# Identity products on TensorE at four waits between the attention and the expert layer of a Perceiver block

## The chip, the cores and the metric

One core of one Trainium2 chip runs the whole kernel. The metric is the device time of one execution in microseconds (us). The engines named below are TensorE (PE in the rows, PEld its weight loads), VectorE (DVE), ScalarE (ACT), GpSimd (POOL) and SyncE (SP), which issues the DMAs.

## The reference

The input x is 2 x 128 tokens of width 512, the context 2 x 2048 tokens. Three blocks follow one another, each with a residual:

```python
x = x + xattn(_layernorm(x), ctx_1024)       # 16 heads of 32, keys and values from the context
x = x + attn(_layernorm(x))                  # self-attention, its own residual and layer norm inside
x = x + ffn(_layernorm(x))                   # 4 experts, top 1
...
# attn: Q, K, V are reshaped (B, S, E) -> (B * H, S, D) without a transpose of heads
out = softmax(Q @ K.T / sqrt(D)) @ V
out = layer_norm(out @ wo + bo + x) * gamma + beta
...
# ffn
expert_idx = argmax(x @ W_router)
h = gelu(x @ W1[e] + b1[e])                  # 512 -> 2048, of the chosen expert
y = layer_norm(h @ Wo + bo + x)
```

## The kernel before

Each engine has one program, written out by hand, and waits on semaphores; nothing is reordered by a scheduler. All data lives at fixed places of SBUF, and PSUM is one array `ps` of 8 banks.

The cross-attention takes the first 356 us and is untouched. Then comes the stretch that this document is about, which has little work for each engine and many hand-overs:

1. `wo` product: TensorE multiplies `attnT` with `wo` for the two halves b of the batch (16 products of 512 columns in the trace). VectorE adds the residual and normalizes to `y`, half by half, with one `pow` on GpSimd each.
2. TensorE transposes `y` (4 per half), ScalarE copies to `yT`, and TensorE makes q, k and v of the self-attention (`qkv`, lines 778, 32 rows each in the trace).
3. Heads are regrouped by copies over 32 partitions: `QT2` by VectorE (L638), `KT2` by VectorE (L648) and ScalarE (L396), `VT2` by ScalarE (L396). `scores2` (L953) needs QT2 and KT2 only.
4. `softmax2(u)` for u = 0 to 7 on VectorE (L658, L659), `exponentials2(u)` on ScalarE (L412), `probs2_T(u)` transposes on TensorE (L963) and their copies on ScalarE (L418). In ScalarE's order the first exponential stands behind all eight VT2 copies of head groups 0 and 1, and four more copies stand behind each of the first two exponentials. Then the transposes of V (L992), `outputs2(0)` (L971, L976), reciprocals and regrouping of its result (L665, L672, L425), the `wo2` product of half 0, `outputs2(1)`, the same again for half 1, and the `wo2` product of half 1.
5. VectorE alone works through the residual, two layer norms and the residual again (L698 to L703, L490), first for half 0 and then for half 1. TensorE transposes each `y` (L772) as it comes, ScalarE copies it, and TensorE makes the router logits (L778, `wr`, 4 columns).
6. VectorE picks the expert (L710 to L717). TensorE spreads the one-hot masks over the partitions (L1024) and transposes them (L1029, `ohT`). VectorE copies `ohT` (L729) behind the splitting of the biases b1 (L725, L727).
7. The expert layer: 16 products with b1 (L1040), whose contraction has only 4 partitions (one for each expert), then 16 tiles of W1 with 24 products of 512 columns each (L1051 to L1053), which VectorE splits into high and low parts two tiles ahead. The output layer and the store follow.

At the very start of the program, TensorE already runs 14 identity products (L863) while the first inputs load; they write to bank `PV_BANK` and nothing reads them. A product of two fp32 operands stands in the trace as two MATMUL records, so these 14 are 28 records.

Of the kernel before, what the change touches and what calls it, by code (L numbers as in the profile page):

```python
# [17 lines left out]
P = 128  # L18
# [5 lines left out]
def perceiver_block(nc, a, out):  # L24
    B, T, D = a["x"].shape
# [4 lines left out]
    HPG = P // DH  # L30
# [17 lines left out]
    with ExitStack() as ctx:  # L48
# [3 lines left out]
        def at(name, shape, dtype, kb):  # L52
            return nc.alloc_sbuf_tensor_at(name, shape, dtype, offset=base + int(kb * KB))

        def sem(name):
            return ctx.enter_context(nc.semaphore(name))
# [19 lines left out]
        ident = at("ident", [P, P], F32, 204)  # L76
# [55 lines left out]
        def cols(n):  # L132
# [25 lines left out]
        ps = ctx.enter_context(nc.psum_tensor("ps", [P, 8, CH], F32))  # L158
        T_BANKS = (4, 5)
        K_BANK, PV_BANK = 6, 7  # L160
# [36 lines left out]
        ones_ready, s2_mm, sub2_done, exp2_done, p2T_mm, pt2_act = (  # L197
            sem(n) for n in ("ones_ready", "s2_mm", "sub2_done", "exp2_done", "p2T_mm", "pt2_act"))
# [569 lines left out]
        def _(pe):  # L768
            def transposes(src, b, bank, sem_out):

                for k in range(KT):
                    last = pe.transpose(ps[:, bank, k * T:(k + 1) * T], src[:, b, k * P:(k + 1) * P], ident[:])  # L772
                last.then_inc(sem_out, 1)

            def product(dst, pairs):

                for n, (l, r) in enumerate(pairs):
                    mm = pe.matmul(dst, l, r, start=(n == 0), stop=(n == len(pairs) - 1))  # L778
                return mm
# [86 lines left out]
            for k in range(KT):  # L866
                if k % HALF == 0:
                    pe.wait_ge(ctx_split, k // HALF + 1)
                for n, (w, t) in enumerate(((wkH, ctxH[0]), (wkL, ctxH[0]), (wkH, ctxL[0]))):
                    last = pe.matmul(ps[:, K_BANK, :], w[:, k, 0:P], t[:, k, :], start=(k == 0 and n == 0),  # L870
                                     stop=(k == KT - 1 and n == 2))
# [62 lines left out]
                    .then_inc(wo_mm, 1)  # L934


            pe.wait_ge(wqkv2_in, 48)
            for b in range(B):
                pe.wait_ge(norm_done, B + b + 1)
                transposes(y, b, 2 + b, yT_mm)  # L940
# [25 lines left out]
            def outputs2(b):  # L966
# [10 lines left out]
                                         start=True, stop=True)  # L977
                last.then_inc(pv2_mm, 1)

            pe.wait_ge(q2_ready, HPG * HPG)  # L980
            pe.wait_ge(k2_dve, 2 * HPG)
            pe.wait_ge(k2_act, 2 * HPG)
# [28 lines left out]


            pe.wait_ge(wr_in, 16)
            for b in range(B):
                pe.wait_ge(norm_done, 2 * B + 2 * (b + 1))
                transposes(y, b, 2 + b, x2T_mm)
                pe.wait_ge(x2T_done, b + 1)
                product(ps[:, 6 + b, 0:E], [(yT[:, k, b * T:(b + 1) * T], wr[:, k, :]) for k in range(KT)])\
                    .then_inc(logit_mm, 1)
# [10 lines left out]
            last.then_inc(ohT_mm, 1)  # L1030


            pe.wait_ge(ohT_ready, 1)
            pe.wait_ge(b1_split, 2)
            pe.wait_ge(mask_done, E // 2)
            pe.wait_ge(yT_lo, B)
            for b in range(B):
                for c in range(IC):
                    for n, part in enumerate((b1H, b1L)):
                        pe.matmul(ps[:, IC * b + c, :], ohT[:, b, :], part[:, c * CH:(c + 1) * CH],  # L1040
                                  start=(n == 0), stop=False)
# [77 lines left out]
```

## Time and profile before

| | |
|---|---|
| median of 3 runs | 601.75 us |
| lowest, highest | 601.21, 604.71 us |
| profiled execution, its whole time | 603.38 us |
| profiled execution, its span | 601.6 us |
| PE busy | 528.6 us, 88% of the span |
| DVE, ACT, POOL busy | 311.2, 184.1, 37.2 us |
| mean granted TensorE clock | 0.933 |

The span runs from the first to the last instruction of the profiled execution; 1.8 us of its whole time lie outside it. A granted clock of 1.00 is 2.4 GHz and 0.50 is 1.2 GHz. All times in the rows count from the start of the span.

### The profile page before, as it was taken

The numbers are of one execution on the slowest core, as the hardware profiler recorded it, in microseconds if no ns is written. First come the engines' busy times: TensorE is split into PE (matmuls) and PEld (weight loads), VectorE is DVE, ScalarE is ACT, GpSimd is POOL, SyncE is SP. The second block draws the span as 40 slices with busy tenths as digits, with TensorE's granted clock in tenths as the row PEclk, the third lists the DMA queues.
The fourth block names the chain that finished last, engine by engine and source line by source line (L and its number), as shares of the span: only waits on it lengthen the run. The fifth ranks groups of instructions, "written<-read, shape, count | busy, mean of one in ns | idle before, by whom it ended". The sixth has DMA issues, their size and how long they took to land.

```text
span 601.6 us, 8656 instructions
## 1 busy us (share of the span) xinstructions
PE 528.6 (88%) x3550; PEld 393.9 (65%) x3550; DVE 311.2 (52%) x561; ACT 184.1 (31%) x282; POOL 37.2 (6%) x32
## 2 busy tenths in 40 slices
PE   6999999999989899999999587934555999999995
PEld 5777767777767688777767455823225788888642
DVE  4545335566756411175757222874286579766122
ACT  3110053737363431136363720493222000000400
POOL 0300000003940000000000000000000000000000
PEclk9999999999989999999999798977765699999999
DMA  8600000004300000300004420000020565542000
GB/s 290 253 0 1 1 1 1 2 2 144 138 0 3 1 0 1 139 3 2 1 1 185 167 99 9 0 3 1 0 70 2 244 246 200 212 173 113 0 8 28
DMA packets 7998, 41.24 MB, mean 69 GB/s; under 512 B 1172, under 2 KB 2196, under 8 KB 4116
## 3 DMA queue, kind: packets, MB, share of 16 engines
q1 hardware_dynamic: 7960, 40.69, 18.3%
q8 instruction: 29, 0.48, 0.3%
q14 instruction: 9, 0.07, 0.0%
HBM read 40.16 MB, written 0.52 MB: 68 GB/s over the span
## 4 chain that ended last, share of the span: by engine, by line
PE 80%; DVE 9%; ACT 5%; issue 3%; DMA 1%; POOL 0%; SPq 0%; POOLq 0%; DVEq 0%; ACTq 0%
PE ps L778 41%; PE ps L835 10%; PE ps L821 6%; PE ps L1051 5%; PE ps L1052 5%; PE ps L1053 5%; PE ps L850 5%; ACT VT L396 2%; DMA wv_raw<-in_xWv 1%; PE ps L1040 1%; DVE rden L665 1%; DVE Pm L526 1%; DVE small L484 1%; DVE cT L672 1%; ACT Pm L325 1%
## 5 line engine op out<-in xcount | busy, mean ns | idle before, releaser
L333 ACT COPY PT<-ps 128x512 f32<-128x512 f32 x96 | 53.3, 588 | 102.0 <-PE ps L835 102.0
L835 PE MATMUL ps<-ident,Pm 128*128 128x128 f32 x512 | 71.1, 282 | 4.9 <-ACT PT L333 2.7
L835 PEld LDWEIGHTS ps<-ident,Pm 128*128 128x128 f32 x512 | 57.8, 143 | 24.9 <-issue 16.9
L526 DVE TENSOR_SCALAR_CACHE_REDUCE Pm<-ps,small 128x512 f32<-128x512 f32 x96 | 66.4, 748 | 8.6 <-PE ps L821 8.6
L325 ACT ACTIVATE Pm<-Pm,small 128x2048 f32<-128x2048 f32 x32 | 64.2, 2006 | 14.2 <-DVE Pm L526 14.2
L778 PE MATMUL ps<-ctxH,wkH 128*128 128x512 f32 x124 | 52.0, 419 | 2.8 <-DVE Kr L506 2.4
L1051 PE MATMUL ps<-w1H,zH 128*128 128x512 f32 x128 | 50.7, 396 | 0.0
L778 PE MATMUL ps<-wvH,ctxH 128*128 128x512 f32 x128 | 50.3, 393 | 0.2 <-DVE wvL L570 0.2
L1052 PE MATMUL ps<-w1L,zH 128*128 128x512 f32 x128 | 50.5, 395 | 0.0
L1053 PE MATMUL ps<-w1H,zL 128*128 128x512 f32 x128 | 50.3, 393 | 0.0
L778 PE MATMUL ps<-wvL,ctxH 128*128 128x512 f32 x128 | 50.0, 391 | 0.0
L778 PE MATMUL ps<-wvH,ctxL 128*128 128x512 f32 x128 | 50.0, 391 | 0.0
L778 PE MATMUL ps<-ctxL,wkH 128*128 128x512 f32 x124 | 49.3, 398 | 0.0
L778 PE MATMUL ps<-ctxH,wkL 128*128 128x512 f32 x124 | 49.0, 395 | 0.0
L506 DVE TENSOR_SCALAR Kr<-ps,small 128x512 f32<-128x512 f32 x32 | 24.0, 750 | 47.1 <-PE ps L778 47.1
L515 DVE COPY V<-ps 128x512 f32<-128x512 f32 x16 | 11.1, 692 | 62.7 <-PE ps L778 62.7
L535 DVE COPY PT<-ps 128x512 f32<-128x512 f32 x32 | 22.1, 692 | 36.4 <-PE ps L835 35.6
L778 PEld LDWEIGHTS ps<-ctxH,wkH 128*128 128x128 f32 x124 | 23.6, 190 | 21.5 <-issue 17.5
L821 PE MATMUL ps<-Kr,qT 32*128 32x512 f32 x256 | 36.5, 640 | 0.6 <-ACT qT L352 0.6
L690 DVE TENSOR_TENSOR w1L<-w1raw,w1H 128x2048 fp32r<-128x2048 f32 x16 | 36.7, 2293 | 0.6
L850 PE MATMUL ps<-PT,V 128*32 128x128 f32 x1024 | 34.6, 276 | 0.9 <-DVE PT L535 0.9
L320 ACT COPY V<-ps 128x512 f32<-128x512 f32 x16 | 9.4, 589 | 77.5 <-PE ps L778 77.5
(151 smaller groups left out, 718.4 us busy)
## 6 DMA issues: line engine op xcount, KB each, us to landing
w1raw<-in_W SPq DMA_DIRECT2D x16, 1024.0 KB, 4.8
raw<-in_ctxT SPq DMA_DIRECT2D x7, 1024.0 KB, 4.9
woF<-in_ffn_Wo SPq DMA_DIRECT2D x1, 4096.0 KB, 14.0
rows<-in_rows SPq DMA_DIRECT2D x6, 256.0 KB, 3.9
raw<-in_ctxT SPq DMA_DIRECT2D x2, 512.0 KB, 6.2
wv_raw<-in_xWv SPq DMA_DIRECT2D x2, 512.0 KB, 8.5
wq<-in_xWq SPq DMA_DIRECT2D x1, 1024.0 KB, 12.9
wo<-in_xWo SPq DMA_DIRECT2D x1, 1024.0 KB, 4.7
```

The lines of the kernel that those rows point to most:

```text
L325: act.activation(Pm[:, i, :], Pm[:, i, :], ACT.Exp, bias=mx[:, p % 2, i, C - 1:C], scale=-1.0, accum_out=den[:, p, i:i + 1]).then_inc(exp_ ...
L333: act.copy(PT[:, c % 2, i, :, :].rearrange("p k t -> p (k t)"), ps[:, T_BANKS[i % 2], :]).then_inc(pt_act, 1)
L506: dve.tensor_scalar(Kr[:, c, :], ps[:, K_BANK, :], bias3[:, 1, p % G:p % G + 1], None, ALU.add).then_inc(k_done, 1)
L526: dve.tensor_scalar(Pm[:, i, c * CH:(c + 1) * CH], ps[:, i, :], -1.0, mx[:, p % 2, i, c - 1:c] if c else NOT_YET, ALU.mult, ALU.min, accum ...
L690: dve.tensor_tensor(w1L[n % 2][:], w1raw[n % 2][:], w1H[n % 2][:].bitcast(F32), ALU.subtract).then_inc(w1_split, 1)
L778: mm = pe.matmul(dst, l, r, start=(n == 0), stop=(n == len(pairs) - 1))
L821: pe.matmul(ps[:, i, :], qT[q, g, b * T:(b + 1) * T], Kr[q, c, :], start=True, stop=True)\
L835: last = pe.transpose(ps[:, T_BANKS[i % 2], j * P:(j + 1) * P], Pm[:, i, c * CH + j * P:c * CH + (j + 1) * P], ident[:])
L850: last = pe.matmul(ps[q, PV_BANK, 0:T], V[:, c * JT + j, (HPG * g + i) * DH:(HPG * g + i + 1) * DH], PT[:, c % 2, i, j, :], start=(c == 0 ...
L1051: pe.matmul(dst, zH[:, n, t], wH[:, cc], start=False, stop=False)
L1052: pe.matmul(dst, zH[:, n, t], wL[:, cc], start=False, stop=False)
L1053: last = pe.matmul(dst, zL[:, n, t], wH[:, cc], start=False, stop=(n == NW1 - 1))
```

## The change

A helper `busy(n)` issues n products of the 128x128 identity with itself into `PV_BANK`, columns 0 to 127. They signal nothing. It is called four times on TensorE:

- 16 products behind the `wo` product, after the wait for the weights `wq2`, `wk2`, `wv2` and ahead of the wait for `y` (call 1);
- 40 products behind q, k and v, ahead of the waits for QT2 and KT2 (call 2);
- 40 products behind the last `wo2` product, after the wait for the router's weights and a further wait for `pt2_act` (the bank holds the last transposed probabilities until ScalarE has copied them; the same count was already awaited ahead of `outputs2(1)`), and ahead of the wait for the normalized tokens (call 3);
- 40 products behind the one-hot transposes, ahead of the waits for `ohT`, b1 and the masks (call 4).

```diff
@@ -934,7 +934,12 @@
+            def busy(n):
+                for _ in range(n):
+                    pe.matmul(ps[:, PV_BANK, 0:P], ident[:], ident[:], start=True, stop=True)
+
             pe.wait_ge(wqkv2_in, 48)
+            busy(16)
             for b in range(B):
                 pe.wait_ge(norm_done, B + b + 1)
                 transposes(y, b, 2 + b, yT_mm)
@@ -977,6 +982,7 @@
                 last.then_inc(pv2_mm, 1)
 
+            busy(40)
             pe.wait_ge(q2_ready, HPG * HPG)
             pe.wait_ge(k2_dve, 2 * HPG)
             pe.wait_ge(k2_act, 2 * HPG)
@@ -1011,6 +1017,8 @@
             pe.wait_ge(wr_in, 16)
+            pe.wait_ge(pt2_act, B * HPG)
+            busy(40)
             for b in range(B):
                 pe.wait_ge(norm_done, 2 * B + 2 * (b + 1))
                 transposes(y, b, 2 + b, x2T_mm)
@@ -1030,6 +1038,7 @@
             last.then_inc(ohT_mm, 1)
 
+            busy(40)
             pe.wait_ge(ohT_ready, 1)
             pe.wait_ge(b1_split, 2)
             pe.wait_ge(mask_done, E // 2)
```

The other engines' programs stay as they are. On TensorE, calls 1 and 2 stand around q, k and v; before:

```order
L778 MATMUL ps<-wo,attnT 128x512 x8
L772 MATMUL ps<-ident,y 128x128 x8
L778 MATMUL ps<-yT,wq_82 128x256 x16
L778 MATMUL ps<-yT,wk_83 128x256 x16
L778 MATMUL ps<-yT,wv_84 128x256 x16
L953 MATMUL ps<-KT_107,QT_106 128x128 x32
```

and now (the scores have moved from L953 to L958 of the file):

```order
L778 MATMUL ps<-wo,attnT 128x512 x8
L939 MATMUL ps<-ident 128x128 x16
L772 MATMUL ps<-ident,y 128x128 x8
L778 MATMUL ps<-yT,wq_82 128x256 x16
L778 MATMUL ps<-yT,wk_83 128x256 x16
L778 MATMUL ps<-yT,wv_84 128x256 x16
L939 MATMUL ps<-ident 128x128 x40
L958 MATMUL ps<-KT_107,QT_106 128x128 x32
```

Everything behind an inserted group on TensorE waits for it to be issued. Calls 3 and 4 stand around the router, again on TensorE; before:

```order
L778 MATMUL ps<-wo_85,cT 128x512 x4
L772 MATMUL ps<-ident,y 128x128 x4
L778 MATMUL ps<-wr,yT 128x4 x4
L1024 MATMUL ps<-ident,small 128x128 x8
L1029 MATMUL ps<-ident,small 4x128 x2
L1040 MATMUL ps<-b1H,ohT 128x512
```

and now:

```order
L778 MATMUL ps<-wo_85,cT 128x512 x4
L939 MATMUL ps<-ident 128x128 x40
L772 MATMUL ps<-ident,y 128x128 x4
L778 MATMUL ps<-wr,yT 128x4 x4
L1032 MATMUL ps<-ident,small 128x128 x8
L1037 MATMUL ps<-ident,small 4x128 x2
L939 MATMUL ps<-ident 128x128 x40
L1049 MATMUL ps<-b1H,ohT 128x512
```

One group now precedes the transposes of half 0 and one the products with b1; the pair of transposes and logits for half 1, not shown twice, has no group ahead of it.

## Rows read from the trace of the kernel before

**Rows 1.** The page: engines' busy time, and the granted clock in 40 slices.

```profile
PE 528.6 (88%) x3550; PEld 393.9 (65%) x3550; DVE 311.2 (52%) x561; ACT 184.1 (31%) x282; POOL 37.2 (6%) x32
...
PEclk9999999999989999999999798977765699999999
```

**Rows 2.** Timeline of TensorE, the 28 identity records at the start.

```profile
start us, us, engine line op out<-in xcount [idle before <-releaser]
1.52 4.42 PE L863 MATMUL ps<-ident 128*128 128x128 f32 x19 [1.52 <-POOL ident L272]
...
5.52 1.49 PE L863 MATMUL ps<-ident 128*128 128x128 f32 x10
```

**Rows 3.** Windows of the stretch: busy time of each engine, granted clock (PEclk).

```profile
core 0: us, PE busy (x) PEld busy (x) DVE busy (x) ACT busy (x) POOL busy (x), PEclk, DMA share, GB/s
...
363.41:367.70 4.29, 1.29 (x9) 0.81 (x8) 2.27 (x5) 0.84 (x2) 0.55 (x1) 1.00 0.02 4
367.80:371.10 3.30, 3.01 (x7) 2.48 (x8) 0.00 (x0) 0.24 (x1) 0.00 (x0) 0.50 0.00 0
...
398.60:408.70 10.10, 5.53 (x25) 4.61 (x24) 4.84 (x8) 9.03 (x17) 0.00 (x0) 0.50 0.00 0
408.75:415.50 6.75, 3.25 (x75) 2.60 (x73) 3.36 (x1) 2.23 (x5) 0.00 (x0) 1.00 0.01 2
415.60:429.15 13.55, 5.62 (x10) 2.67 (x11) 4.05 (x11) 5.38 (x12) 0.00 (x0) 0.50 0.00 0
...
446.30:449.60 3.30, 0.65 (x3) 0.11 (x2) 2.47 (x6) 0.00 (x0) 0.55 (x1) 1.00 0.10 42
449.70:461.27 11.57, 5.63 (x24) 4.65 (x22) 5.92 (x19) 2.15 (x4) 1.10 (x2) 0.50 0.00 1
461.27:465.28 4.01, 4.00 (x18) 3.62 (x18) 3.98 (x4) 0.77 (x2) 0.00 (x0) 0.50 0.01 4
466.24:473.36 7.12, 7.12 (x16) 5.10 (x16) 7.09 (x6) 0.74 (x1) 0.00 (x0) 0.50 0.07 16
473.36:476.94 3.58, 3.58 (x9) 2.82 (x9) 0.83 (x1) 0.00 (x0) 0.00 (x0) 0.50 1.02 407
477.20:562.00 84.80, 84.80 (x376) 70.21 (x375) 56.32 (x36) 3.86 (x7) 0.00 (x0) 1.00 0.52 191
```

**Rows 4.** Timeline of TensorE from the wo product to the expert layer.

```profile
363.41 0.63 PE L772 MATMUL ps<-ident,y 128*128 128x128 f32 x4
366.76 0.66 PE L772 MATMUL ps<-ident,y 128*128 128x128 f32 x4 [2.72 <-DVE y L490]
368.09 8.68 PE L778 MATMUL ps<-yT,wq 128*128 128x256 f32 x32 [0.67 <-ACT yT L388]
376.60 7.07 PE L778 MATMUL ps<-yT,wk 128*128 128x256 f32 x32
383.51 7.07 PE L778 MATMUL ps<-yT,wv 128*128 128x256 f32 x32
392.98 2.07 PE L953 MATMUL ps<-KT,QT 32*128 32x128 f32 x64 [2.40 <-DVE KT L648]
...
424.65 5.93 PE L778 MATMUL ps<-wo,cT 128*128 128x512 f32 x8 [2.85 <-ACT cT L425]
...
440.18 6.69 PE L778 MATMUL ps<-wo,cT 128*128 128x512 f32 x8 [7.72 <-ACT cT L425]
449.52 0.95 PE L772 MATMUL ps<-ident,y 128*128 128x128 f32 x4 [2.65 <-DVE y L490]
...
456.30 1.12 PE L772 MATMUL ps<-ident,y 128*128 128x128 f32 x4 [3.28 <-DVE y L490]
458.09 1.87 PE L778 MATMUL ps<-wr,yT 128*128 128x4 f32 x8 [0.68 <-ACT yT L388]
461.28 3.79 PE L1024 MATMUL ps<-ident,small 128*128 128x128 f32 x16 [1.32 <-DVE small L717]
```

**Rows 5.** Timeline of ScalarE and VectorE, what the stretch waits for.

```profile
395.55 0.68 DVE L658 TENSOR_REDUCE small<-ps 128x4 f32<-128x512 f32 x1
397.38 0.63 ACT L412 ACTIVATE P<-P 128x512 f32<-128x512 f32 x1
407.52 0.59 ACT L449 COPY V<-ps 128x512 f32<-128x512 f32 x1 [0.58 <-PE ps L992]
408.38 0.59 ACT L449 COPY V<-ps 128x512 f32<-128x512 f32 x1 [0.27 <-PE ps L992]
...
460.06 0.17 DVE L710 COPY small<-ps 128x4 f32<-128x4 f32 x1 [3.75 <-PE ps L778]
```

## The prediction

> **What bounds the kernel now.** I read the page first: TensorE is busy for 88% of the span, and its granted clock is near full in most slices but 0.5 to 0.7 in slices 26 to 32, from about 390 to 480 us [rows 1]. That is the stretch in which TensorE works in short bursts. The windows of that stretch then show at which stage the clock is down [rows 3]: after 367.8 (in q), from 398.6 to 408.7, from 415.6 to 429.1, and, but for three microseconds from 446.3, up to the tenth product of W1 at 477. From there TensorE is busy without a gap at full clock to the end of the W1 tiles, so whatever delays or hastens the first W1 products moves the end of the kernel by the same amount. Last I read the timeline for what releases each burst [rows 4, 5]. TensorE runs in a chain with ScalarE and VectorE here, so that products issued in a wait are free only as long as they end before the wait does. The waits at the four places are 2.72 us (366.76; the first half of y is ready at once), 2.40 us (392.98), 2.65 us (449.52) and, behind the masks, from 465.28 to 466.24, 0.96 us [rows 3, 4].
>
> **What one identity product costs.** The same instruction stands at the start [rows 2]. 19 records take 4.42 us; less the tail of the last (0.42) and a slower first step (0.16) that is 18 steps of 0.213 us, so 0.427 us a product at 1.2 GHz. The last 10 records take 1.49 us: two slow steps of 0.213, the tail of 0.275 and seven steps of 0.112, so 0.224 us a product at 2.4 GHz. (The clock column has no record for these first microseconds; the steps show the level.) These rows also show that identity products alone bring the clock up: it rose after 4.4 us of them. So 16 take 3.7 us and 40 take 9.1 us at 2.4 GHz with the slower first step, 17.2 us at 1.2 GHz. Every group of 40 is more than three times as long as the wait that it stands in.
>
> **Call 1 (16 products).** They start at 363.41, where now the transposes of half 0 stand, and end at 367.1. The second half of y comes at 366.71 and no longer decides. Transposes of half 0 and then half 1, 0.44 us each, start at 367.1 and 367.5. From the start of the second transposes to q takes 1.33 us today (366.76 to 368.09) [rows 4], so q starts at 368.85, 0.75 us later. Against that the clock: q takes 8.51 us to the start of k, k takes 6.91 us to the start of v. The difference of 1.6 us is the price of one short fall of the clock (the slow window from 367.8 to 371.1 [rows 3]). With TensorE busy up to 367.9 I take it that this fall is gone. Together **-0.85 us**; bounds +0.75 (the clock falls all the same) and -1.6.
>
> **Call 2 (40 products).** v is issued by 383.51 + 6.91 = 390.42, now 389.57. Plus 9.1 the group ends at 398.7, and the scores start there and not at 392.98: 5.7 us late. What of this reaches the chain is read at ScalarE: its first exponential starts at 397.38 although VectorE had subtracted the maximum by 395.6 (its next instruction starts at 395.55 [rows 5]), since ScalarE has VT2 copies to do until then. Now the exponential follows the scores by the same 2.65 us as VectorE's result, at 401.35. That is 3.95 us late with call 1, so call 2 costs **+4.8 us**: 1.75 of its delay is hidden behind ScalarE's copies. ScalarE paces the steps behind it one by one, so these 3.95 us go on unchanged to outputs2(0), VectorE's reciprocals, both wo2 products and the layer norms. Can the group pay back? The clock is still at 2.4 GHz during the scores today, and between the scores and the next full burst TensorE has the same gaps as before, in which it fell today. I count nothing. Bounds: -0.85 if the transposes of V run at 2.4 GHz (ScalarE's idle 0.58 and 0.27 ahead of its copies [rows 5]), +1.7 if the following outputs2 products, which had 2.4 GHz today [rows 3], run at half of it.
>
> **Call 3 (40 products).** The last wo2 product is issued by 446.7, now 450.65. It brought the clock up just before its end today (446.3 [rows 3]), so the group runs at 2.4 GHz and ends at 459.8. Half 0 was ready at 449.5 (now 453.5) and waits 6.3 us, but the chain needs half 1, which VectorE delivers at 456.25, now 460.2. From 459.8: transposes of half 0 until 460.24, logits 0.22 + 0.64 us later (from the end of the transposes over ScalarE's copy) at 461.1, eight records of 0.112 until 462.0, transposes of half 1 until 462.4, logits from 463.3 to 464.2, read by VectorE at 464.4. Today that read starts at 460.06 [rows 5], so without this group it would be at 464.0. **+0.4 us**; bound +3 if the clock falls within these small pieces, each then twice as long, and -1.3 if the group ended well ahead of half 1.
>
> **Call 4 (40 products).** Today the masks and one-hot transposes are issued from 461.28 to 465.28 at 1.2 GHz, and b1 starts at 466.24 [rows 3, 4]. Between call 3 and the masks TensorE has more idle than busy time, as in the 11.6 us ahead of the masks today, so I take it that the masks run at 1.2 GHz again. With 4.0 us of masks straight ahead of it, and 4.4 us of identity products needed at the start [rows 2], the group may begin slow: I add 0.8 us, which is half of its first 1.6 us at 1.2 GHz (bounds 0 and 1.7). The group ends 9.1 + 0.8 us behind 465.28, at 475.2 in today's times: **+8.95 us** for b1. Against that, the 16 records of b1 take 7.12 us at 1.2 GHz to the start of W1, and at the 0.226 us of the long window (84.80 us for 375) 3.6 us: **-3.5 us**. The first nine records of W1 take 3.84 us to 477.20 and then 2.0: **-1.8 us**.
>
> Does the clock hold through b1? The rows speak against it: TensorE was busy without a gap in b1 for 7.1 us, longer than the 4.4 us that sufficed at the start, and the clock stayed at 1.2 GHz; it rose only 3.6 us into W1 [rows 2, 3]. Products over 4 partitions do not raise it, and I take it that they do not hold it either, so that it falls in or just behind b1 for one short stretch, at the price that q shows: **+1.6 us** (bounds 0 and 3.4, for a stretch twice as long). The Trainium skill, page "TensorE: Matmul & The Clock Gate", Part 1, says that the clock gate follows how busy the PE has been; by it b1 would hold the clock, and the sum would be 1.6 us lower. This trace, with busy PE and 1.2 GHz in b1, does not agree.
>
> VectorE and the DMAs have the W1 tiles ready earlier than TensorE wants them now: two tiles are split ahead, and VectorE is busy for 56.3 of 84.8 us in that part [rows 3]. So nothing is added there. The new wait for pt2_act repeats one that outputs2(1) has already passed: nothing.
>
> **Sum.** -0.85 + 4.8 + 0.4 + 8.95 - 3.5 - 1.8 + 1.6 = **+9.6 us** against the profiled execution of 603.38 us: 613.0. The median of the runs shown is 1.6 us lower, 601.75, so I predict **611.3 us**. The three runs differ by 3.5 us among themselves, so about 1% (6 us) is what a measurement of this kernel can tell from no change.
>
> **The rivals.**
>
> *The clock holds from call 3 on* (0.15). Masks and one-hot transposes, 18 records, are then 18 x 0.101 = 1.8 us shorter, the slow start of call 4 (0.8) and the fall behind b1 (1.6) go: +9.6 - 4.2 = +5.4 us, 607.1 us. For it: less idle time than today between call 3 and the masks. Against it: b1.
>
> *The clock holds through b1 only* (0.12), as the page's rule has it: +8.0 us, 609.7 us.
>
> *More falls* (0.15). Call 3 finds small pieces at 1.2 GHz (+1), the fall comes inside b1 and lasts twice as long (+1.7), and outputs2(0) runs slow (+1.2): +13.5 us, 615.2 us.
>
> *The other side: the groups carry 2.4 GHz over every gap* (0.06). Then also the wo2 product of half 0, on the chain with 5.86 us of issue at mostly 1.2 GHz, takes 3.5 (-2.35), the transposes of V give 0.85, and at call 3 the group ends before half 1 comes, whose transposes and logits at 2.4 GHz save 1.3 in place of costing 0.4 (-1.7). +5.4 - 2.35 - 0.85 - 1.7 = +0.5 us, 602.3 us, not slower. It decides at the gap behind the scores: the clock must still be up at 424.65, over 13 us in which today it fell twice [rows 3]. No call stands in that gap, which speaks against it.
>
> *The products do not raise or hold the clock* (0.02): at 1.2 GHz each group of 40 would last 17.2 us, 8 us more than counted above, and the time would be over 630 us; the steps of the first group of rows on L863 nearly exclude it [rows 2].
>
> **How the numbers follow.** The forecast has 0.50. The range reaches from just under the clock that holds from call 3 on to just short of the case of more falls: 606.5 to 614.5. Slower by over 1% (over 607.8): 0.50 + 0.12 + 0.15 + 0.02 and a third of 0.15, less a little for a run that falls luckily: 0.80. Within 1%: 0.18. Faster by over 1%: 0.02.
>
> **What would show each step.** In the profile after: 32 records of L939 that end near 367.1 and q at 7 us (call 1); scores near 398.7 and the first L412 near 401.4 (call 2); the L710 read of half 1 some 4.4 us later than 460.06 (call 3); a wait of TensorE ahead of b1 that is gone, b1 at 0.226 us a record and a stretch at 1.2 GHz early in W1 (call 4). The prediction is wrong above all if the clock behaves otherwise between the calls, or if an identity product takes other than 0.224 us at 2.4 GHz.

## The result and the profile after

The changed kernel takes 610.82 us (median of 4 runs, 609.75 to 611.95) against 602.56 us for the kernel before beside it: a ratio of 1.0134 with a 95% interval of 1.0093 to 1.0175. It is slower by 1.3%, as forecast; 611.3 us had been predicted. The profiled execution took 611.76 us, its span 610.0 us.

The page of the changed kernel, its busy times and granted clock, answers to [rows 1]:

```profile
PE 549.1 (90%) x3822; PEld 418.3 (69%) x3822; DVE 311.3 (51%) x561; ACT 184.0 (30%) x282; POOL 37.2 (6%) x32
...
PEclk9999999999989999999999699977778899999998
```

TensorE is busy for 20 us more and the mean clock rose from 0.933 to 0.954, and the kernel is slower all the same. Neither number says what is on the chain. The timeline of TensorE after the change does, beside [rows 4]:

```profile
357.09 7.10 PE L778 MATMUL ps<-wo,attnT 128*128 128x512 f32 x16 [1.05 <-issue]
364.03 3.73 PE L939 MATMUL ps<-ident 128*128 128x128 f32 x32
367.60 1.04 PE L772 MATMUL ps<-ident,y 128*128 128x128 f32 x8
369.37 7.17 PE L778 MATMUL ps<-yT,wq 128*128 128x256 f32 x32 [0.73 <-ACT yT L388]
376.38 7.07 PE L778 MATMUL ps<-yT,wk 128*128 128x256 f32 x32
...
390.19 9.09 PE L939 MATMUL ps<-ident 128*128 128x128 f32 x80
399.21 2.07 PE L958 MATMUL ps<-KT,QT 32*128 32x128 f32 x64
...
450.29 9.09 PE L939 MATMUL ps<-ident 128*128 128x128 f32 x80
459.22 0.60 PE L772 MATMUL ps<-ident,y 128*128 128x128 f32 x4
...
461.41 0.64 PE L772 MATMUL ps<-ident,y 128*128 128x128 f32 x4
462.72 1.05 PE L778 MATMUL ps<-wr,yT 128*128 128x4 f32 x8 [0.68 <-ACT yT L388]
465.10 3.48 PE L1032 MATMUL ps<-ident,small 128*128 128x128 f32 x16 [1.32 <-DVE small L717]
...
468.80 9.14 PE L939 MATMUL ps<-ident 128*128 128x128 f32 x80
```

The four groups stand there as 32, 80, 80 and 80 records. The waits for the second half of y (ahead of q), ahead of the scores and ahead of b1 are gone from the list: what stood there is now the group, and longer. ScalarE's first exponential shows the other side, a wait that it did not have in [rows 5]:

```profile
401.91 0.63 ACT L412 ACTIVATE P<-P 128x512 f32<-128x512 f32 x1 [4.74 <-DVE P L659]
```

The windows of the changed kernel around the router and the expert layer answer to [rows 3]; the number behind the column of POOL is the granted clock:

```profile
448.50:465.40 16.90, 14.23 (x111) 12.63 (x110) 10.86 (x29) 2.15 (x4) 2.19 (x4) 1.00 0.18 64
465.60:468.80 3.20, 3.20 (x17) 3.03 (x16) 3.17 (x4) 0.77 (x2) 0.00 (x0) 0.50 0.00 0
468.95:477.80 8.85, 8.85 (x81) 8.79 (x79) 8.82 (x8) 1.53 (x2) 0.00 (x0) 1.00 0.10 20
477.86:481.70 3.84, 3.84 (x17) 2.85 (x16) 0.15 (x1) 0.00 (x0) 0.00 (x0) 1.00 1.15 491
482.60:485.80 3.20, 3.20 (x9) 2.53 (x8) 0.00 (x0) 0.00 (x0) 0.00 (x0) 0.50 0.76 328
```

All but the first 0.4 us of the masks run at 1.2 GHz, group 4 and b1 at 2.4, and then the clock falls once more, 0.8 us into W1, for 3.4 us.

The 14 profiled executions of this document start the wo product at 354.3 to 358.9 us, although no kernel here touches what stands ahead of it; the clock falls at slightly different places in the cross-attention, which is the likely reason. So all that follows is counted from the start of the wo product (356.46 before, 357.09 after), as the lateness of a step against the kernel before:

| step | lateness forecast | in the trace |
|---|---|---|
| q starts | +0.75 | +0.65 |
| k starts | -0.85 | -0.85 |
| first exponential | +3.95 | +3.90 |
| outputs2(1) starts | +3.95 | +4.40 |
| logits of half 1 read (L710) | +4.35 | +3.19 |
| b1 starts | +13.3 | +10.99 |
| first W1 product | +9.8 | +7.74 |
| 31st W1 product | +9.6 | +7.69 |

From the 31st W1 product on the difference does not change (the last one is at +7.7). With the 0.6 us that the two wo products stand apart these make the 8.4 us between the two spans; the medians are 8.3 us apart.

### The profile page after: what moved, and what is told of

Read it like the earlier page. It is cut to its first block, busy times and chain, and to the rows that moved or that the text cites. A ratio compares the mean times of both kernels' runs of the same rounds, so it can differ in the third digit from the quotient of the medians.

```text
span 610.0 us, 9199 instructions
## 1 busy us (share of the span) xinstructions
PE 549.1 (90%) x3822; PEld 418.3 (69%) x3822; DVE 311.3 (51%) x561; ACT 184.0 (30%) x282; POOL 37.2 (6%) x32
## 4 chain that ended last, share of the span: by engine, by line
PE 85%; DVE 5%; ACT 4%; issue 2%; DMA 1%; SPq 0%; POOLq 0%; DVEq 0%; ACTq 0%
PE ps L778 41%; PE ps L835 10%; PE ps L821 6%; PE ps L939 5%; PE ps L1060 5%; PE ps L1061 5%; PE ps L1062 5%; PE ps L850 5%; DMA wv_raw<-in_xWv 1%; DVE rden L665 1%; DVE Pm L526 1%; ACT cT L425 1%; ACT VT L396 1%; PE ps L1049 1%; ACT Pm L325 1%
## 5 line engine op out<-in xcount | busy, mean ns | idle before, releaser
L688 DVE CAST w1H<-w1raw 128x2048 fp32r<-128x2048 f32 x16 | 19.6, 1225 | 28.6 <-PE ps L1062 28.5
```

## The experiments

Each total is the ratio to the kernel before on the same chip, with its 95% interval. All edits are to the changed kernel unless the text says otherwise.

**Each call alone.** The other three calls are taken out, and the added wait with call 3. For call 1 alone:

```diff
-            busy(40)
             pe.wait_ge(q2_ready, HPG * HPG)
...
-            pe.wait_ge(pt2_act, B * HPG)
-            busy(40)
             for b in range(B):
...
-            busy(40)
             pe.wait_ge(ohT_ready, 1)
```

> Only the 16 identity products ahead of the transposes of y. My theory: they cost 0.75 us to the start of q and save 1.6 us because the clock no longer falls at the start of q, so 0.8 us less than the kernel before, with q at 7.0 us to the start of k. Rival (the group is only a delay): the clock falls in q all the same and the time is 0.8 us more. Both are below what the total alone resolves, so the start of q and of k in the trace decide.

Ratio 0.9996 (0.9967 to 1.0024). The total cannot tell it from nothing, the timeline can:

```profile
365.25 3.73 PE L939 MATMUL ps<-ident 128*128 128x128 f32 x32
...
370.58 7.17 PE L778 MATMUL ps<-yT,wq 128*128 128x256 f32 x32 [0.73 <-ACT yT L388]
377.59 0.59 PE L778 MATMUL ps<-yT,wk 128*128 128x256 f32 x2
```

q takes 7.01 us to the start of k; q starts 0.64 late and k 0.86 early, in every run with call 1. The runs without it scatter: q takes 8.51 us before, 9.17 in the run with call 2 alone, 9.15 with call 4 alone, 9.13 in the later run with fillers at the wo2 product, and 7.01 with call 3 alone, where the clock happened not to fall. Counted from the wo product, k starts 19.28 us behind it with call 1, and 20.14 (before), 21.26, 21.24 and 21.23 us without it where the clock fell, 18.65 where it did not. So call 1 gains 0.86 to 2.0 us where the clock would have fallen, and loses 0.6 where it would not.

> Only the 40 identity products ahead of the scores. My theory: scores 6.6 us late, first exponential 4.8 us late, and nothing of it is given back up to the router: 4.8 us more than the kernel before. Rival (the group hides in the wait of 2.4 us and in the slack of ScalarE): at most 2 us more.

Ratio 1.0108 (1.0058 to 1.0158). k started 1.1 us later in this execution than before, for q's clock. Against that start, the scores are 6.45 us late (403.01) and the exponential 4.75, as its rows say, TensorE first and ScalarE second:

```profile
393.99 9.09 PE L939 MATMUL ps<-ident 128*128 128x128 f32 x80
403.01 1.17 PE L957 MATMUL ps<-KT,QT 32*128 32x128 f32 x32
```

```profile
405.70 0.63 ACT L412 ACTIVATE P<-P 128x512 f32<-128x512 f32 x1 [4.74 <-DVE P L659]
```

The lateness is still 4.3 us at W1. The rival, a group hidden in slack, is out.

> Only the 40 identity products behind the last wo2 product, with the added wait. My theory: the logits are read 0.4 us later to 1.3 us earlier; the total is within 1.5 us of the kernel before, less if the masks keep 2.4 GHz. Rival (every group of 40 costs its length less its wait of 2.65 us): 6 us more.

Ratio 0.9984 (0.9957 to 1.0012). Between the start of the wo2 product of half 1 and the reading of the logits 0.35 us are added, where +0.4 was forecast; the rival's 6 us are out. Here the clock fell inside the logits of half 1 and stayed down for the masks (456.7 to 463.5), but rose at the start of b1, which it had not done before. From b1 to the 31st W1 product takes 13.96 us and not 15.73. So a group that costs 0.35 us where it stands went with a gain of 1.8 us further on in this execution, since the clock turned at another place; the total, with its interval of over 3 us, cannot show it.

> Only the 40 identity products ahead of the b1 products. My theory: b1 starts 8 to 9 us late, b1 and the first W1 products give back 5, the clock falls once more just behind b1 at 1.6 us: 4.0 to 5.3 us more than the kernel before. Rival (b1 holds the clock): no fall, 2.4 to 3.7 us more. Rival (the warmed clock pays for the group): no more than the kernel before.

Ratio 1.0118 (1.0081 to 1.0154). b1 starts 8.9 us later against the reading of the logits, as forecast. The group takes 9.88 us to b1, its first 1.8 us at 1.2 GHz. But the windows show more clock lost than the theory had:

```profile
467.10:477.10 10.00, 10.00 (x82) 9.49 (x81) 7.00 (x6) 0.00 (x0) 0.00 (x0) 1.00 0.41 157
477.30:484.00 6.70, 6.70 (x16) 4.77 (x15) 0.00 (x0) 0.00 (x0) 0.00 (x0) 0.50 1.00 430
```

The clock fell in the middle of b1 (475.10 to 480.43) and was down for 6.8 us, the upper bound of the prediction. The W1 products are 7.1 us late (8.55 less 1.4 by which this execution was late ahead of the group already, 1.1 of it for q's clock) and not 4.0 to 5.3, so the theory of this run was mis-sized by the longer fall. Both rivals are out.

**What holds the clock.**

```diff
-            busy(40)
+            for _ in range(40):
+                pe.matmul(ps[:, PV_BANK, 0:P], ident[0:E, :], ident[0:E, :], start=True, stop=True)
             pe.wait_ge(ohT_ready, 1)
```

> As the changed kernel, but the 40 products of call 4 multiply the first 4 partitions of the identity only, so that their contraction is as narrow as that of b1. My theory (products over 4 partitions do not hold the clock): the clock falls to 1.2 GHz within the group, which then lasts 12 to 17 us and not 9.1, and b1 and the first W1 products run at 1.2 GHz: 7 to 12 us more than the changed kernel. Rival (a busy TensorE holds the clock, whatever it multiplies): the group lasts 9.1 us and the time is that of the changed kernel.

620.1 us, ratio 1.029 (1.0208 to 1.0372), 9.3 us over the changed kernel. The group's row and its windows, with b1 (third window) and the first W1 products (fourth):

```profile
466.81 14.45 PE L1042 MATMUL ps<-ident 4*128 4x128 f32 x80
```

```profile
466.81:470.00 3.19, 3.19 (x29) 3.19 (x29) 3.19 (x4) 1.59 (x2) 0.00 (x0) 1.00 0.00 0
470.30:480.90 10.60, 10.60 (x52) 10.60 (x51) 5.55 (x4) 0.00 (x0) 0.00 (x0) 0.50 0.66 249
480.92:488.00 7.08, 7.08 (x18) 5.02 (x17) 0.00 (x0) 0.00 (x0) 0.00 (x0) 0.50 0.86 370
488.01:493.90 5.89, 5.89 (x15) 4.63 (x15) 0.00 (x0) 0.00 (x0) 0.00 (x0) 0.50 0.00 0
```

TensorE is busy in every microsecond of these windows, and the clock falls 3.3 us into the group and stays down for 23.9 us, until W1 has run for 6 us. With 128 partitions the same count of products at the same place held 2.4 GHz to the end. That settles it: products over 4 partitions (narrow ones from here on) neither hold nor raise the clock, and a busy TensorE is not enough.

**The slack at the scores.**

```diff
-            busy(40)
+            busy(16)
             pe.wait_ge(q2_ready, HPG * HPG)
```

> As the changed kernel, but with 16 products in place of 40 in call 2. They take 3.7 us in a wait of 2.6, so the scores are 1.2 us late. My theory (up to 1.75 us of lateness hides behind ScalarE's copies): the first exponential comes as in the run with call 1 alone, and the total is 4.8 us less than the changed kernel. Rival (the whole lateness of the scores counts): 5.4 us less minus nothing hidden, with the exponential 1.2 us later than in the run with call 1 alone, so 3.7 us less than the changed kernel.

Ratio 1.0062 (1.0030 to 1.0093), 606.29 us, 4.5 us less than the changed kernel (4.3 by the ratios). That lies between the theory's 4.8 and the rival's 3.7, and the intervals cover both; the trace decides. The scores are 1.11 us later than with call 1 alone, the exponential 0.03 us: ScalarE goes over from its copies to it without idle time.

```profile
391.69 3.85 ACT L396 COPY VT<-vF 32x256 f32<-32x256 f32 x6
395.56 0.63 ACT L412 ACTIVATE P<-P 128x512 f32<-128x512 f32 x1
```

**b1 among the W1 products.** Half 0 of b1 stays a block; each pair of half 1 moves ahead of its first W1 product.

```diff
+                        if n == 0 and b:
+                            biases(b, c)
                         pe.matmul(dst, zH[:, n, t], wH[:, cc], start=False, stop=False)
```

> As the changed kernel, but the b1 products of the second half of the batch are issued among the first W1 products of that half, so that no more than eight narrow products stand in a row. My theory: the clock no longer falls behind b1, and W1 is 1.6 us further on: 1.6 us less than the changed kernel. Rival (the fall has another cause, such as the end of the groups): it falls at the same place and the time is unchanged.

Ratio 1.0129 (1.0074 to 1.0184): no gain, and yet the theory's first half holds. The clock does not fall:

```profile
479.56:487.50 7.94, 7.94 (x29) 4.80 (x29) 0.00 (x0) 0.00 (x0) 0.00 (x0) 1.00 1.05 455
```

From b1 to the 25th W1 product takes 11.11 us, in the changed kernel with its fall 11.07. What the fall no longer costs goes to the changes between wide and narrow products:

```profile
482.19 0.39 PE L1066 MATMUL ps<-w1H,zL 128*128 128x512 f32 x1
482.51 0.49 PE L1048 MATMUL ps<-b1H,ohT 4*128 4x512 f32 x1
482.84 0.39 PE L1048 MATMUL ps<-b1L,ohT 4*128 4x512 f32 x1
483.17 0.50 PE L1064 MATMUL ps<-w1H,zH 128*128 128x512 f32 x1
483.50 0.40 PE L1065 MATMUL ps<-w1L,zH 128*128 128x512 f32 x1
```

These four steps take 1.31 us where four of 0.227 make 0.91, and so four times (1.31 to 1.33). A change between products over 128 and over 4 partitions costs some 0.2 us, in the step to the new kind and in the one behind it, and eight of them (1.6 us) eat what one fall costs.

**Groups cut to the waits.** Calls of 16, 0, 30 and 12 products, and 5 more ahead of the masks, these into a free bank.

```diff
-            def busy(n):
+            def busy(n, bank=PV_BANK):
...
+            busy(5, O2_BANKS[0])
             pe.wait_ge(z_ready, 1)
...
-            busy(40)
+            busy(12)
             pe.wait_ge(ohT_ready, 1)
```

> The groups cut to the waits: 16 products in call 1, none in call 2, 30 in call 3, 5 more ahead of the masks, 12 in call 4. My theory: -0.85 (call 1), -1.3 (logits of the second half at 2.4 GHz), b1 starts when it would have without any group and it and the first W1 products run at 2.4 GHz (-5.3), the fall behind b1 costs 1.6: 5.9 us less than the kernel before, about 1%. Rival (12 products are too few, the clock is down at b1): 2.1 us less.

Ratio 0.9975 (0.9947 to 1.0003), 2.1 us gained at the last W1 product. The number is the rival's, the cause is not: 12 products were not too few, b1 starts at 2.4 GHz (464.89). The clock fell at 453.7, in the small pieces around the second logits, and again in b1 at 467.4. The 5 products ahead of the masks ran at 1.2 GHz, took 2.27 us (457.42 to 459.69) and held the masks back by 0.8 us.

**The wo2 product of half 0.** The four calls are out; fillers stand elsewhere.

```diff
             for u in range(HPG + 1, B * HPG):
+                if u == B * HPG - 1:
+                    busy(31, O2_BANKS[0])
                 probs2_T(u)
             pe.wait_ge(wo2_in, 16)
+            busy(11, O2_BANKS[0])
```

> None of the four groups; 31 identity products ahead of the transposes of the last probabilities (in a wait of 7.6 us) and 11 ahead of the wo2 product of half 0 (in a wait of 2.85 us), into a free bank. My theory (the clock can be carried over a long gap at no cost, and this product is on the chain): the wo2 product of half 0 runs at 2.4 GHz, 3.5 us and not 5.8 to its successor, and all behind it comes 2.3 us earlier. Rival (the chain gives it back, the wo2 product is covered): the logits come no earlier.

Ratio 0.9930 (0.9904 to 0.9955). The rows of TensorE, against 5.86 us from the wo2 product to its successor before:

```profile
411.88 7.09 PE L939 MATMUL ps<-ident 128*128 128x128 f32 x62
419.66 0.66 PE L967 MATMUL ps<-ident,P 128*128 128x128 f32 x4 [0.68 <-ACT P L412]
420.15 2.62 PE L939 MATMUL ps<-ident 128*128 128x128 f32 x22
423.64 3.67 PE L778 MATMUL ps<-wo,cT 128*128 128x512 f32 x8 [0.87 <-ACT cT L425]
427.25 1.08 PE L975 MATMUL ps<-PT,V 128*32 128x128 f32 x32
```

3.61 us, 2.25 us less, and the fillers delay nothing, since both waits still end with idle time. The total gained more, 4.1 us. The profiled execution is 2.85 us ahead at the last W1 product, and its rows say of what: 2.25 us at the wo2 product, 1.7 us from b1 to the 31st W1 product (14.02 us and not 15.73, since the clock rose at 462.9, just ahead of b1), less 1.1 us that q lost to its clock. That the chain gives the 2.25 us back is refuted: they stand unchanged at the logits. Whether the fillers bring the early rise, and whether the other executions had it, no run shows.

**All of it.** The two fillers of the run before, 16 products in call 1, none in call 2, smaller groups around the router, 12 ahead of b1, and b1 mixed.

```diff
+                if b:
+                    busy(13)
                 pe.wait_ge(norm_done, 2 * B + 2 * (b + 1))
                 transposes(y, b, 2 + b, x2T_mm)
+                busy(3)
                 pe.wait_ge(x2T_done, b + 1)
```

> All fillers cut to fit: 16 in call 1, none in call 2, the two of the run before this one, and around the router 11, 3, 13, 3 and 5 products in each gap in place of one group, 12 ahead of b1, and b1 of the second half among the first W1 products. My theory: -0.85 (q), -2.35 (wo2 product of half 0), -1.3 (logits at 2.4 GHz), -5.3 (b1 and W1 at 2.4 GHz, without the fall): 9.8 us less than the kernel before up to W1, a ratio of about 0.984. Rival (short fillers do not hold the clock over the router as the group of 30 did not): the clock falls before the masks and once more in b1, and the ratio is 0.992.

Ratio 0.9939 (0.9912 to 0.9966), worse than the filler for the wo2 product alone (0.9930), though not beyond the intervals. The clock fell at 455.9 in the logits of half 1 and stayed down over the masks (to 462.8), as the rival had it; the second fall that it expected, in b1, did not come. The 5 products ahead of the masks, at 1.2 GHz, held them back by 0.8 us again. The 12 products ahead of b1 now come late and hold b1 back until 465.73, 1.5 us behind the moment at which `ohT` is ready (4.96 behind the masks, as before).

In the next run the gaps around the router are filled more closely, and b1 is one block again:

```diff
-            busy(11)
+            busy(15)
             for b in range(B):
                 if b:
-                    busy(13)
+                    busy(18)
...
-            busy(12)
+            busy(11)
             pe.wait_ge(ohT_ready, 1)
```

> As the spread run, with fillers that leave smaller gaps around the router (15, 3, 18, 3, 5 products), 11 ahead of b1, and b1 in its old place as one block. My theory (the clock fell ahead of the masks in the spread run since the gaps around half 1 were too wide): the masks run at 2.4 GHz, b1 starts 5 us behind them and 4.6 us earlier than in the kernel before, counted from the wo product; b1 to the 24th W1 product takes 11.1 us and not 14.4 (one fall behind b1 included). In all 7.8 us less than the kernel before, ratio 0.987. Rival (the logits, 4 columns wide, bring the clock down whatever stands beside them): the clock falls ahead of the masks as in the spread run, ratio 0.993.

596.77 us, ratio 0.9900 (0.9872 to 0.9927), the lowest of all, though its interval meets that of the filler for the wo2 product alone. The windows from the last wo2 product over the masks (second) and b1 (third):

```profile
444.00:457.90 13.90, 13.47 (x113) 12.57 (x111) 8.66 (x25) 2.15 (x4) 1.64 (x3) 1.00 0.05 18
457.94:462.90 4.96, 4.73 (x40) 4.49 (x40) 4.92 (x6) 2.46 (x3) 0.00 (x0) 1.00 0.00 0
462.91:466.50 3.59, 3.59 (x16) 2.85 (x16) 3.56 (x4) 0.00 (x0) 0.00 (x0) 1.00 0.02 5
466.70:469.90 3.20, 3.20 (x8) 2.46 (x8) 3.20 (x3) 0.00 (x0) 0.00 (x0) 0.50 0.09 20
```

The logits did not bring the clock down once the gaps beside them were filled; that rival is out. b1 has its old wait for `ohT` again (0.24 us), so nothing is in its way, and the fall at the end of b1 is there as expected. The 7.8 us forecast came to 6.1 in the medians. In the profiled execution the missing 1.6 us stand at outputs2(0), which found the clock down:

```profile
408.67 1.94 PE L976 MATMUL ps<-PT,V 128*32 128x128 f32 x32 [0.92 <-ACT PT L418]
410.35 1.86 PE L981 MATMUL ps<-PT,ones 128*32 128x128 f32 x32
```

It takes 3.47 us to the next transposes (412.14), 1.89 in the kernel before. None of the groups covers this fall.

The last run adds to it the split of b1 in two blocks:

```diff
                 for b in range(B):
+                    if n == 0 and b:
+                        biases(b)
                     t = slice(b * T, (b + 1) * T)
```

> As the run before this one, with the eight b1 products of the second half as one block between the two halves of the first W1 tile. Two changes between narrow and wide products are added where the mixed run had eight, at about 0.1 to 0.15 us each. My theory: no fall behind b1, 1.6 less 0.3, so 1.3 us less than the run before this one, ratio 0.985. Rival (the fall is only moved, or the blocks of eight are enough for one): no difference.

Ratio 0.9920 (0.9894 to 0.9946), by the totals not told apart from the run before it. Two falls, behind each block of eight, in the second and fourth window:

```profile
460.49:463.60 3.11, 2.95 (x12) 2.10 (x13) 3.11 (x3) 0.00 (x0) 0.00 (x0) 1.00 0.00 0
463.80:467.00 3.20, 3.20 (x9) 2.34 (x7) 3.17 (x3) 0.00 (x0) 0.00 (x0) 0.50 0.02 5
467.20:470.40 3.20, 3.20 (x14) 2.31 (x14) 1.23 (x2) 0.00 (x0) 0.00 (x0) 1.00 0.88 353
470.60:473.80 3.20, 3.20 (x9) 2.55 (x8) 0.00 (x0) 0.00 (x0) 0.00 (x0) 0.50 0.85 369
```

The theory of this run falls. From b1 to the 31st W1 product takes 14.62 us, against 12.35 with one block; that the medians do not show it fits outputs2(0), which ran at 2.4 GHz in this execution (1.88 us). Eight narrow products in a row can be enough for a fall, but need not be: in the mixed run and in the one with everything a block of eight stood ahead of W1 too, and no fall came. What decides between the two is not shown.

## Why the prediction was right

The total came out nearer (611.3 against 610.82) than the sum deserves: the sum had +9.6 us, the medians are 8.3 us apart, and the traces 7.7 us counted from the wo product. The kernel before measured 602.56 us beside the changed one, and not the 601.75 that the forecast started from. Direction, mechanism and most terms held; two terms, calls 3 and 4, were mis-sized, and that the total hides it is luck.

*The price of a product* held: 9.02 us from the start of group 2 to the scores (9.1 forecast).

*Call 1* came out as worked out (-0.85), but it is counted against one execution. The gain hangs on a fall of the clock that one of the five profiled executions without call 1 did not have, and that cost three others more.

*Call 2* cost 4.75 us (-0.85 to +3.90) where 4.8 was forecast, and the slack behind ScalarE's copies is there: the scores were delayed by 6.46 us and the exponential by 4.75, so 1.7 was hidden, and in the run with 16 products all of the 1.11 us was. The 0.5 us added up to outputs2(1) is the wo2 product of half 0 (6.37 us and not 5.86), a rise of the clock that came later (434.7); the sum had left it at nothing.

*Call 3* was mis-sized: -1.2 us from outputs2(1) to the logits and not +0.4. The wo2 product ahead of it ran at 2.4 GHz for its last part and took 5.08 us, so the group ended at 459.22, ahead of the second half of y (461.28), and the logits of half 1 ran at 2.4 GHz. That is the bound of -1.3 which the prediction gave for just this case; alone, where the wo2 product took 6.44 us, the call cost 0.35.

*Call 4* was mis-sized in its first term: b1 was 7.80 us later (10.99 - 3.19), not 8.95. The masks were 0.3 us faster, as the clock fell only within them, and group 4 ran at 2.4 GHz from its first record: the 0.8 us for a slow start were not there, though they were with call 4 alone (9.88 us against 9.06). b1 gave back 3.25 us of 3.5. The fall behind b1 was forecast from the 4 partitions of b1, and it came at the place named and for 3.4 us. The run with 4 partitions in the group shows the cause. That its length is not fixed (6.8 us with call 4 alone) was inside the bounds.

The terms with their measured values: -0.85 + 4.75 + 0.5 - 1.2 + 7.8 - 3.25 - 0.05 = +7.7 us, against +9.6.

*The rivals.* That the clock holds from call 3 on came true for a part only: it stood at 2.4 GHz from 448.4 to 465.5, through both logits, and fell 0.4 us into the masks. That it holds through b1 and W1 is refuted. *More falls* did not come here; one of its parts, the fall inside b1 that lasts twice as long, came with call 4 alone. That the groups carry 2.4 GHz over every gap did not happen: it fell at 404.0, 421.1 and 441.6. That the products do not raise or hold the clock is refuted by the 9.02 and 9.06 us of groups 2 and 4. The two groups of 31 and 11 products show that it can be carried over one of these gaps, if the group stands in the gap itself.

The calls are not independent. The totals do not show it (the four ratios alone add up to +2.1%, together they make +1.3%, and the intervals are too wide to tell these apart), but the traces do: from the reading of the logits to the 31st W1 product call 4 costs 7.1 us alone and 4.5 with the others. The masks are 0.3 us faster, group 4 starts fast (0.8), and alone call 4 ran into the longer fall (1.5).

## What to carry to other kernels

Filler products are free only while they end before the wait that they stand in does. Read the wait's length and the price of one filler at both levels of the clock (here 0.224 and 0.427 us), count the products from them, and put them in the gap directly ahead of a product on the chain that runs at 1.2 GHz. Here 42 of them, fitted into two gaps ahead of one wo2 product, went with a kernel 0.7% faster, and 136 in groups longer than their waits with one 1.3% slower. Where the fillers themselves may find 1.2 GHz, count them at the slow price: five of them took 2.3 us ahead of the masks and held these back. Then look at what the products behind are: narrow ones (4 partitions) lose the clock again (16 in a row did in all seven traces in which they started at 2.4 GHz), whatever was spent to raise it. Last, count the fall of the clock as something that differs from one execution to the next; a gain that hangs on one of them is read from several traces, not from one.

## What the runs showed of the hardware

Products over 4 partitions let the granted clock fall from 2.4 to 1.2 GHz while TensorE is busy without a gap (at 470.1, 3.3 us into such products) and do not raise it again in the 17.9 us up to W1; the same count of identity products over all 128 partitions at the same place held it for 9.1 us, and with call 4 alone it rose 1.8 us into them.

Changing between products over 128 and over 4 partitions costs about 0.2 us each time (in the mixed run 1.31 us against 0.91 for four steps with two changes).

Transposes of fp32 tiles by the identity can raise the clock: in the kernel before it rose at 408.7 behind 4.2 us of transposes alone (the clock of these windows is in [rows 3]).

```profile
404.51 2.12 PE L963 MATMUL ps<-ident,P 128*128 128x128 f32 x8 [2.11 <-ACT P L412]
406.43 1.91 PE L992 MATMUL ps<-ident,VT 128*128 128x128 f32 x8
408.13 0.89 PE L963 MATMUL ps<-ident,P 128*128 128x128 f32 x4
```
 The Trainium skill, page "TensorE: Matmul & The Clock Gate", Part 4, says that full rate does not engage for its transpose mode. For these transposes, issued by the program as such, the trace does not agree; which mode the engine was in for them, no row shows.
